# A two-layer transformer on one core: the feed-forward and second layer of a batch walked between the attention steps of the next

## What is computed

```python
x = _layernorm(x + softmax_attention_with_rope(x))      # 16 heads of 8
x = _layernorm(x + top4_of_16_experts(x) + shared_swiglu(x))
x = _layernorm(x + linear_attention(x))                  # features (elu(.) + 1), 16 heads, 32 features each
x = _layernorm(x + x @ W.T + b + top2_of_8_lora_gates(x))
```

```python
q_prime = (elu(q @ random_matrix) + 1) / 16;  k_prime = (elu(k @ random_matrix) + 1) / 16
kv = einsum('bhsm,bhsd->bhmd', k_prime, v);   k_sum = k_prime.sum(2)
out = (q_prime @ kv) / maximum(q_prime @ k_sum, 1e-6)
```

## Time and profile before

| what | value |
|---|---|
| median of the runs | 628.48 us (627.59 to 629.42) |
| span of the profiled execution | 623.1 us |
| PE busy, 2872 matmuls | 499.6 us, 80% |
| DVE busy, 1015 instructions | 404.9 us, 65% |
| ACT busy, 276 instructions | 214.9 us, 34% |
| POOL busy, 101 instructions | 109.1 us, 18% |
| mean granted TensorE clock | 0.868 |

### The profile page before, as it was taken

The page is one execution under the profiler, slowest core; times in us unless marked ns, Lnnn a source line. Parts: engine busy times, 40 slices in busy tenths (PEclk is TensorE's granted clock), DMA queues, the critical chain, the costliest instruction groups (busy, mean ns, idle before and its releaser), DMA issues. The chain is left out here.

```text
span 623.1 us, 7805 instructions
## 1 busy us (share of the span) xinstructions
PE 499.6 (80%) x2872; PEld 235.1 (38%) x2872; DVE 404.9 (65%) x1015; ACT 214.9 (34%) x276; POOL 109.1 (18%) x101
## 2 busy tenths in 40 slices
PE   5142993299975999379989989999999999988962
PEld 2010230133322334133334355444554565654651
DVE  6663773088852899349797588977556656656454
ACT  0100262065642666236546712232232313223210
POOL 9770000075050510001000000000000100111120
PEclk9565597599996999769999999999899979968775
DMA  2221328101110011100000000000000000000001
GB/s 97 77 105 65 108 72 197 81 10 52 48 81 26 2 52 66 82 10 2 2 2 2 1 1 1 0 2 0 1 1 1 1 0 1 1 18 0 18 1 34
DMA packets 9422, 20.58 MB, mean 33 GB/s; under 512 B 2082, under 2 KB 7336, under 8 KB 8680
## 3 DMA queue, kind: packets, MB, share of 16 engines
q1 hardware_dynamic: 9384, 20.08, 9.5%
HBM read 15.68 MB, written 4.19 MB: 32 GB/s over the span
## 5 line engine op out<-in xcount | busy, mean ns | idle before, releaser
L1010 DVE TENSOR_REDUCE negmax<-psum 128x1 f32<-128x512 f32 x256 | 169.5, 685 | 101.5 <-PE psum L465 100.6
L734 ACT ACTIVATE probs<-psum 128x1024 f32<-128x1024 f32 x128 | 126.8, 1023 | 163.3 <-PE psum L481 161.2
L465 PE MATMUL psum<-KS,QS 96*128 96x512 bf16 x256 | 104.7, 420 | 38.0 <-DMA QS<-parts_dram 29.7
L481 PE MATMUL psum<-QS,KS 99*128 99x512 bf16 x256 | 80.2, 398 | 46.4 <-DMA QS<-maxp 46.2
L500 PE MATMUL psum<-probs,VA 128*32 128x256 f32 x1024 | 84.8, 397 | 0.6 <-ACT probs L734 0.6
L708 PE MATMUL psum<-xT,late 128*128 128x512 f32 x144 | 71.7, 622 | 0.0
L465 PEld LDWEIGHTS psum<-KS,QS 96*128 96x128 bf16 x256 | 25.6, 100 | 121.7 <-DVE negmax L1010 59.6
L389 POOL TENSOR_SCALAR var<-mv 128x4 f32<-128x4 f32 x16 | 3.7, 229 | 286.6 <-DVE mv L906 286.5
L481 PEld LDWEIGHTS psum<-QS,KS 99*128 99x128 bf16 x256 | 24.8, 102 | 69.5 <-DMA QS<-maxp 47.1
L870 DVE TENSOR_TENSOR QS<-QS,psum 128x512 f32<-128x512 f32 x64 | 43.7, 682 | 2.4 <-PE psum L708 0.4
L829 ACT ACTIVATE QS<-psum 128x512 f32<-128x512 f32 x36 | 21.5, 597 | 65.6 <-PE psum L708 65.6
(11 more groups left out here) (150 smaller groups left out, 599.6 us busy)
## 6 DMA issues: line engine op xcount, KB each, us to landing
KS<-parts_dram SPq DMA_DIRECT2D x3, 1152.0 KB
QS<-parts_dram SPq DMA_DIRECT2D x9, 384.0 KB
parts_dram<-parts SPq DMA_DIRECT2D x8, 384.0 KB, 2.9
late<-in_late SPq DMA_DIRECT2D x1, 2956.0 KB, 15.1
out_y<-KS SPq DMA_DIRECT2D x4, 256.0 KB, 2.2
...
QS<-maxp SPq DMA_DIRECT2D x48, 4.0 KB, 1.7
```

Source lines behind the costliest of these rows:

```text
L465: mm(sm_bank(u)[:, :], QS[b % 2][0:KROW, h, qt * P:(qt + 1) * P], KS[b % 2][0:KROW, h, :], start=True, stop=True).then_inc(sm_full, 1)
L481: last_ = mm(ps[2 * hf + j][:, :], KS[b % 2][0:KROW + 3, h, kt * P:(kt + 1) * P], QS[b % 2][0:KROW + 3, h, :], start=True, stop=True)
L734: fn(probs[:, n % 2, 2 * hf:2 * hf + 2, :], psum[:, 2 * hf:2 * hf + 2, :], ACT.Exp, scale=float(DH) ** -0.5).then_inc(exp_done, 1)
L1010: V.tensor_reduce(out=negmax[:, G % 4, i:i + 1], in_=sm_bank(u)[:, :], axis=X, op=ALU.max, negate=True).then_inc(sm_free, 1)
```

## The change

One function, `walk_of_work`, makes one list of steps that all engines walk. Step t has the scores of unit t (`S`), the scores for the maximum of unit t + 24 (`M`, `LOOK`), every fourth step a `PV`, and what `TEMPLATE` places: positions are counted in steps from the end of the own batch's scores, so the feed-forward of a batch (steps 20 to 51) stands between the attention steps of the next batch, and its layer 2 (58 to 110) between those of the next and the one after. For the last batch both stand alone.

```diff
+TEMPLATE = ((5, "heads", 0), (6, "heads", 1), (7, "heads", 2), (8, "heads", 3), (10, "attnT", 0), (12, "proj", 0),
+            (15, "norm0", 0), (18, "resT", 0), (19, "gate", 0), (27, "combine", 0),
+            (52, "chunk", 0), (54, "norm1", 0), (58, "x2T", 0), (59, "kT", 0), (60, "qT", 0), (61, "V", 0),
+            (62, "K", 0), (63, "Kv", 0), (64, "K", 1), (65, "Kv", 1), (66, "Q", 0), (67, "Qv", 0), (67, "KV", 0),
+            (68, "Q", 1), (69, "Qv", 1), (71, "O", 0), (72, "O", 1), (75, "AT", 0), (77, "Y1", 0), (80, "norm2", 0),
+            (83, "x3T", 0), (92, "lg", 0), (104, "ghT", 0), (106, "Y2", 0), (109, "norm3", 0), (110, "save", 0))
+
+
+def walk_of_work():
+
+    at = defaultdict(list)
+    for b in range(NB):
+        own, base = HG * NT * NG * b, HG * NT * NG * (b + 1)
+        if b == 1:
+            for off, kind, i in ((-22, "rope", 0), (-21, "rope", 1), (-20, "rope", 2), (-19, "rope", 3), (-10, "split", 0),
+                                 (-4, "split", 1), (-3, "store", 0), (3, "store", 1), (8, "val", 0)):
+                at[off].append((kind, b, i))
+        if b >= 2:
+            for off, kind, i in ((11, "rope", 0), (12, "rope", 1), (13, "rope", 2), (14, "rope", 3), (15, "val", 0),
+                                 (16, "split", 0), (19, "split", 1), (20, "store", 0), (24, "store", 1)):
+                at[own - 64 + off].append((kind, b, i))
+        if b:
+            for g in range(NG):
+                at[own - 64 + 27 + 16 * g].append(("stacks", b, g))
+        at[own + 20].append(("bout", b, 0))
+        for off, kind, i in TEMPLATE:
+            at[base + off].append((kind, b, i))
+        for k in range(PAIRS):
+            g = base + (23 + 3 * k if k else 20)
+            at[g].append(("G", b, k))
+            at[g + 1].append(("U", b, k))
+            if k:
+                at[g + 2].append(("D", b, k - 1))
+                at[g + 2].append(("C", b, k))
+        at[base + 51].append(("D", b, EP))
+    for i, t in enumerate((1, 3, 8, 11, 13)):
+        at[t].append(("late", 0, i))
+
+    order = []
+    for t in range(-LOOK, max(at) + 1):
+        if 0 <= t < UNITS:
+            order.append(("S", t, 0))
+        u = t + LOOK
+        if u < UNITS:
+            order.append(("M", u, 0))
+            if u % 16 == 15:
+                order.append(("mx", u // 16, 0))
+        if u % 16 == 2 and 16 <= u < UNITS + 16:
+            order.append(("max", u // 16 - 1, 0))
+        if t % 4 == 2 and 6 <= t <= UNITS + 2:
+            order.append(("PV", t // 4 - 1, 0))
+        if t % 16 == 3 and 16 < t < UNITS + 16:
+            order.append(("OU", t // 16 - 1, 0))
+        order += sorted(at[t], key=lambda s: s[0] not in ("G", "U", "C", "D"))
+        order.append(("step", t, 0))
+    return order
```

```diff
+            def store_group(b, i, g):
+
+                src = parts[32 * g:32 * (g + 1), i, :, :]
+                for n in range(3):
+                    if i == 0:
+                        dst = stack_dram[b, 0, g, 24 * n:24 * (n + 1)].rearrange("(p d) j t -> p (d j) t", p=3)
+                    else:
+                        dst = stack_dram[b, 1, g].rearrange("(p n d) j t -> p n (d j) t", p=3, n=3)[:, n]
+                    sp.dma_start(dst.rearrange("p c t -> c p t"), src).then_inc(stack_st[g], 16)
+
+            def load_group(b, g):
+                sp.wait_ge(stack_st[g], 96 * (b + 1))
+                if b:
+                    sp.wait_ge(s_full, 64 * (b - 1) + 16 * (g + 1))
+                else:
+                    sp.wait_ge(init_pool, 2)
...
+                    dst = (KS, QS)[i][0:KROW, HG * g:HG * (g + 1), :].rearrange("r h t -> r (h t)")
+                    sp.dma_start(dst, stack_dram[b, i, g].rearrange("r j t -> r (j t)")).then_inc(qk_ld[g], 16)
...
             def load_max(G):
                 sp.wait_ge(maxp_done, G + 1)
-                if G >= 2:
-                    sp.wait_ge(maxrow_ld[G % 2], 48 * (G // 2))
+                if G >= NG:
+                    sp.wait_ge(s_full, 16 * (G - NG + 1))
```

The split of the maxima and the norm's subtract and multiply move from VectorE to GpSimd:

```diff
+            def split_max(G):
+
+                o = mpart[:, G % 2, :]
+                v = negmax[:, G % 4, :]
+                pool.wait_ge(sm_free, 16 * (G + 1))
+                if G >= 2:
+                    wait_full(pool, ("max", G - 2, 0))
+                link(G_.tensor_scalar(o[:, 0:16], v, 1.0, None, ALU.mult))
+                link(tt(mrest[:, :], v, o[:, 0:16], ALU.subtract))
+                link(G_.tensor_scalar(o[:, 16:32], mrest[:, :], 1.0, None, ALU.mult))
+                tt(o[:, 32:48], mrest[:, :], o[:, 16:32], ALU.subtract).then_inc(mpart_done, 1)
+
...
-                tt(rstd[:, b, :], var[:, b, :], minus_half[:, :], ALU.pow).then_inc(rstd_done[k], 1)
+                link(G_.tensor_scalar(var[:, b, :], mv[:, b, :, 1], LN_EPS, None, ALU.add))
+                link(tt(rstd[:, b, :], var[:, b, :], minus_half[:, :], ALU.pow))
+                for t in range(NT):
+                    ins = G_.tensor_scalar(res[:, b * NT + t, :], z_of(k, b)[:, t, :], mv[:, b, t, 0:1],
+                                           rstd[:, b, t:t + 1], ALU.subtract, ALU.mult)
+                ins.then_inc(res_done[k], 1)
```

```diff
+                    pe.wait_ge(qk_ld[g], 32 * (b + 1))
+                if u >= 2:
+                    pe.wait_ge(sm_free, u - 1)
+                mm(ps[2 + u % 2][:, :], QS[0:KROW, h, qt * P:(qt + 1) * P], KS[0:KROW, h, :],
                    start=True, stop=True).then_inc(sm_full, 1)
...
+                if t % 16 == 0:
+                    pe.wait_ge(maxrow_ld[G % 2], 48 * (G // 2 + 1))
+                if t >= 2:
+                    pe.wait_ge(exp_done, t - 1)
+                mm(ps[t % 2][:, :], KS[0:SROW, h, kt * P:(kt + 1) * P], QS[0:SROW, h, :],
+                   start=True, stop=True).then_inc(s_full, 1)
...
+            def features(b, i):
+
+                for half, u in enumerate((("Ka", b, i), ("Kb", b, i))):
+                    wait_free(pe, u)
+                rows = (slice(0, 64), slice(64, 128))
+                for t in range(2):
+                    for half, u in enumerate((("Ka", b, i), ("Kb", b, i))):
+                        k = slice((2 * i + t) * P, (2 * i + t + 1) * P)
+                        ins = mm(bank_of(u)[:, t * 256:(t + 1) * 256], kT[rows[half], k], c_["rbd"][rows[half], :],
+                                 start=True, stop=True, tile_position=(64 * half, 0))
+                        if t == 1:
+                            ins.then_inc(fullness(u), 1)
+
```

`exps` takes one unit per instruction. A feature is now max(x, 0) + exp(-relu(-x)), by four instructions of ScalarE per round and two of VectorE:

```diff
+            def exp_below_zero(kind, b, i):
+
+                pair = ((kind + "a", b, i), (kind + "b", b, i))
+                first = 8 * b + 4 * (kind == "Q") + 2 * i
+                for half, u in enumerate(pair):
                     wait_full(act, u)
-                    act.wait_ge(split_done[m // 2], 3 * a)
-                    fn(rot[:, m, :], bank_of(u)[:, :], ACT.Identity, bias=c_["b_rope"][:, m:m + 1]).then_inc(rot_done, 1)
-                if kind == "O":
+                    if first + half >= 2:
+                        act.wait_ge(feat_done, first + half - 1)
+                    fn(eneg[:, half, :], bank_of(u)[:, :], ACT.Relu, scale=-1.0).then_inc(act_chain, 1)
+                    n[0] += 1
+                for half, u in enumerate(pair):
+                    act.wait_ge(act_chain, n[0] - 1 + half)
+                    fn(eneg[:, half, :], eneg[:, half, :], ACT.Exp, scale=-1.0).then_inc(exp1_done, 1)
```

1207 lines of the change are left out of this document (486 added, 721 removed).

## The result

The changed kernel takes **695.61 us** (median of four runs, 690.04 to 699.97), the kernel before took 628.04 beside it (627.43 to 629.42). The ratio is 1.108, 95% interval 1.100 to 1.117. The forecast was 590 us and faster, the range ended at 630: wrong in the sign and by 106 us.

What follows compares the result with a forecast made beforehand. TensorE bound the kernel, with losses in attention transfer waits (46 us), a late start and a chained last stage. First exponential at 50, attention 405 to 455, tail 130 to 585, plus 5.4 outside the span: 590 us; range 545 to 630.

Steps and rivals of the forecast that it cites:

- attention alone: Attention without moved work: 250 us once 46 us of maximum-row waits are removed, less 9 for values in one piece.
- moved in, with waits: Work moved into the attention, 128 us, plus new waits of 15, 16 and 5 us.
- tail: After the attention: 64 us for feed-forward 3 with layer 2 of batch 2, then 66 for layer 2 of batch 3.
- I charge all of it: Attention: PE is nearly full, so three feed-forwards and two layers 2 cost their whole 128 us.
- B: Rival, whole kernel: engines fill each other's gaps, waits (1) and (2) hide, tail loses 10; 524 us, chance 0.15.
- (1): Layer 1's transposes wait for POOL's ropes and norm: 6 us at batches 0 and 1, 15 us in all.
- (2): Feature rounds in the attention: the chain through ACT and DVE costs 2 us more per round, 16 us in all.
- (3): Routing chain in steps 19 to 27, where DVE is the longer: 5 us for batch 2's.
- row halves: Feature rounds: two half-height matmuls run side by side, 0.86 us a round instead of 1.72.
- A: Rival, attention steps: ScalarE gates them, scores wait for exponentials; 65 us more, 655 us, chance 0.10.
- C: Rival, attention transfers: DMA waits stay, stores delay maximum rows, 3 us at each of 12 groups; 626 us, chance 0.10.
- D: Rival, norms: POOL is the chain, norms cost 1.5 us more each and DVE's routing is held up; 615 us, chance 0.12.

Runs made afterwards that it cites:

- e3: Changed kernel with only the offsets table altered: gating, feed-forward and layer 2 of all batches behind the attention, batch by batch; 767.24 us, ratio 1.227.
- e18: e16 with the rope pairs of batches 2 and 3 each placed behind a split of the row maxima, in two gaps; 607.26 us, ratio 0.964.
- e2: Changed kernel with 75 matmuls added whose result nobody reads, where TensorE waits; 712.00 us, ratio 1.139.
- e5: Changed kernel with the norm's subtraction and multiplication on VectorE and the ropes of batches 2 and 3 earlier; 659.63 us, ratio 1.057.
- e16: Changed kernel, norm arithmetic on VectorE, feed-forwards and layers 2 staggered behind attention, gates and routing between its steps, later norms and gates, slower routing; 624.82 us, ratio 0.995.

## Why the prediction was wrong

In short: two steps failed. The prediction took 46 us of transfer waits out of the attention and put too little in their place, because it did not cost what the GpSimd queue and the routing hold up; and it charged TensorE's work at the durations of a stretch at a clock of 0.94, while the changed kernel had a mean of 0.784. Against the profile of after, with e3 to part attention from moved work (in e3 the same attention has nothing between its steps but the heads, the projection and the norm of layer 1):

| term | predicted | measured | how |
|---|---|---|---|
| start | 50 | 54.5 | first exponential |
| attention alone | 241 | 281.4 | e3: 54.2 to 335.6 |
| moved in, with waits | 164 | 195.3 | 531.2 - 54.5 - 281.4 |
| tail | 130 | 166.1 | 531.2 to 697.3 |
| sum | 585 | 697.3 | |

**Start.** Right within its bounds: the first M came at 27.20 us (27.5 forecast), the exponential 4.5 us late.

**Attention alone** was the largest miss, and most of it has nothing to do with what moved in. First a reading: the attention before ends with the last exponential at 353, not at 362; two feed-forward matmul groups already stand at 355.5 and 359.7. Like for like the forecast of this row was 232, and the miss is 49 us, in two halves. One is idle time: without the 46 us PE was idle 11 us in the old attention, and it is idle 36 in e3's. Of these, 19.3 are the norm of layer 1 on GpSimd (up to 8.8 each) and 4.3 its splits of the maxima: the things that stand in one GpSimd queue, ropes, norm and split, put new waits where the old ones went. The other half is busy time: 246 us, where 230 before less the 9 for the values would be 221. The values did save their 9 us (83.5 to 74.4), but the score matmuls took 426 and 431 ns in the mean where they took 396 and 403; no run parts the rest. I had counted the norm's waits among the moved work, and only ropes before norm; the split of the maxima, which moved to GpSimd and gates the scores 24 units later, was costed at the start alone (5 us; it was 6.5). e18 put a price on it in the later stages, 19 us in an order that had two waits of 8.5. (The table puts the waits at layer 1's norm, 15 us of the forecast, with the moved work, while e3 has them in the attention; that shifts some of the loss between these two rows, not the sum.)

**Moved work.** The FFN and features at their TensorE time, 128 us, was the step "I charge all of it". It held in kind: B, the engines filling each other's gaps, would have made it less. It failed in that this time was taken from a stretch at a clock of 0.94. From the first to the last exponential PE is busy 404.3 us in the changed kernel and 245.6 in e3: the difference, 158.7 us at a mean clock of 0.84, is what the moved work took, not 128. `KV` is the clearest example: 3.49 us in the earlier trace rows, and with the same 32 records twice that in after's tail, at a granted clock of 0.50,

```profile
536.95 7.05 PE L583 MATMUL psum<-VK,KF 128*128 128x36 f32 x32 [2.95 <-ACT OU L665]
...
569.96 1.08 PE L550 MATMUL psum<-early,res 128*128 128x128 f32 x4 [6.17 <-POOL res L396]
...
587.26 0.59 PE L558 MATMUL psum<-identb,cparts 128*48 128x128 bf16 x4 [4.96 <-DVE cparts L788]
...
628.53 1.09 PE L550 MATMUL psum<-early,res 128*128 128x128 f32 x4 [6.86 <-POOL res L396]
```

**Waits.** (1), ropes then norm, was right in mechanism and short in size: GpSimd's instruction is 0.799 us, not 0.37 to 0.6, the longest wait 8.8, not 6, and the sum between the exponentials 23.4, not 15.

```profile
L396 POOL TENSOR_SCALAR res<-z,mv,rstd 128x128 f32<-128x128 f32 x64 | 50.2, 799 | 1.7
```

On VectorE it was 0.338. Here the Trainium skill (GPSIMD Engine Reference, Engine selection), which says to keep elementwise work on VectorE, points the right way; that the two are about level with one input, as the prediction read it, does not hold for this instruction, at 2.4 times. (2), a feature round, was right in mechanism: 2.12 us idle against 2 forecast in the first, here at the high clock, then 1.9 and 1.4, so 11 us in the attention and not 16 (and its terms add up to 4.0, not 4.5):

```profile
236.37 1.13 PE L486 MATMUL psum<-late,kT 64*128 64x256 f32 x8
237.53 1.08 ACT L675 ACTIVATE eneg<-psum 128x512 f32<-128x512 f32 x2 [1.66 <-PE psum L486]
239.16 1.29 DVE L982 SCALAR_TENSOR_TENSOR KF<-psum,eneg 128x512 f32<-128x512 f32 x2 [0.40 <-ACT eneg L679]
...
240.60 1.13 PE L486 MATMUL psum<-late,kT 64*128 64x256 f32 x8 [2.12 <-DVE KF L982]
```

(3), the routing, was costed at 5 us for one batch. PE's waits for row maxima between the exponentials are 21.3 us against 4.8 before, and the longest, 3.3 us, stand where the routing stands, at 164.7 and 319.9.

The row halves do run side by side, as I took them: the four matmuls of 256 columns of a round (two records each) take 1.13 us; one behind the other, at half of the 0.86 that 512 columns take, they would be 1.72.

**Tail.** Layer 2 of batch 3 alone was costed at 66 us from its `x2T`, and took 68.8 (628.5 to 697.3). The other term, 64 us for feed-forward 3 with layer 2 of batch 2, took 97: 56 of them before batch 3's routing weights at 587.3, with `KV` and `O` at 7 us each and three waits of 3.5 to 6.2. Its PE time was 69 us at a clock of 0.72, where 50 were forecast, and its idle time 28, where 14 were. So both steps failed here too, the durations at the high clock and the waits of the chain.

**Rivals.** A (ScalarE gates the steps) had the right side at 0.10 by the wrong mechanism: PE's scores wait 1.5 us for exponentials beside other engines' 46.8 and 23.5. The time refutes B, and the 1.8 us of waits for maximum rows refute C. D named the right engine and 25 us of it, and still came out faster than before. The rival that was missing is D with the clock: the prediction said it would be wrong "if the granted clock in the middle falls below 0.9", and gave that no price and no chance. It was 0.80 to 0.87 in the stages, where the old attention had 0.89 and what stood behind it 0.90; by e2's count the clock is worth some 43 us of busy time.

**What stays open.** How the remaining loss of e5 (659.63) against the kernel before splits between the chains of layer 2 in the attention, the row maxima behind the routing and the clock: no run held the clock without adding work, and the places of ropes and routing that helped in e16 and e18 were not tried in the interleaved order. And whether the norm on GpSimd would cost anything in e18's order wasn't tried.
